# Row scores over the full array, a new order of first transfers, and layer 1 over whole tiles in a fused attention and feed-forward kernel

## Chip, cores, metric

One core of a Trainium2 chip. The metric is the device time of one execution in microseconds; the kernel before was timed three times.

## What is computed

For 8 batches of 512 tokens with 256 features: attention with 16 heads of 16, softmax over all keys and a triangular mask after it, a residual and a layer norm; a second residual and norm; then a gated feed-forward network with ternary weights, and a last norm. Cut to what matters:

```python
qk = einsum('bhqd,bhkd->bhqk', q, k) / sqrt(s)      # s = 512, 16 heads of 16
p = softmax(qk, axis=-1) * triu(ones((s, s)))       # masked after the softmax
x = embedded + einsum('bhqk,bhkd->bhqd', p, v)      # then a norm with gamma, beta
x = layernorm(x0 + attn(x0))
h = silu(tlin(x, w1)) * tlin(x, w2)                 # 256 -> 1024, twice
h = gelu(tlin(h, h1)); h = gelu(tlin(h, h2))        # 1024 -> 1024
x = layernorm(x + tlin(h, w3))                      # 1024 -> 256
```

## The kernel before

All engines run one hand-written program in program order, joined by semaphores. Each batch goes through attention, norms and feed-forward; the next batch's projections and row scores are placed into the feed-forward of the current one.

**Data split.** Values are kept as a rounded high half and a rest (`hi`, `lo`), so each feed-forward product is done twice. Q and K of a batch are stored to DRAM (`store_rows`) and loaded again as *stacks* `ST` of high and low halves, 64 rows for one head, four heads to a group (`QUAD`), four groups (`NQUAD`), two buffers (`group % 2`).

**Row scores** (`row_scores`, product L964) are there only for the maximum over keys of each query: TensorE makes scores with queries on partitions, VectorE takes the negated maximum (`row_max`, L714 for batches 1 to 7, L722 for batch 0). Here the stacks lie in a layout of their own (`load_rows`), two heads one above the other: rows 0 to 63 and rows 64 to 127 are two products in two halves of the array, into different banks. A *unit* is six or four such products (`SPANS`: three or two query tiles for each of the two sides), 12 units a batch, all on banks 0 to 5, each waiting for the maxima of the one before. Units stand at steps `UNIT_AT` (every 8 of the 128 steps of layers 2 and 3; a step is one k, that is a product with `hi` and one with `lo`), `beside` puts them in. For batch 0 there are 16 units of four, with two extra stacks `RST`.

**Turning the maxima** (`turn_max`, L980 and L981, at steps 54 and 108): 32 columns of maxima for 8 heads are transposed, split into high and low (`split_max`), stored (`store_max`) and loaded as rows 64 and 65 of the transposed stacks (`load_max`), whose partner rows are ones.

**Transposed scores** (`scores_T`, L995): products of 66 rows with keys on partitions, maximum already subtracted; ScalarE's exp reads them (L623). Groups 0 to 3 are loaded again in the transposed layout (`load_stacks(..., True)`). Then come the products with the values (L1014, L1021, L1027), normalizing (`take_z`), two norms (`first_norm`, `second_norm`) for each of four token tiles.

**Layer 1.** The normalized x is transposed in two parts, tokens 0 to 383 and 384 to 511 (`turn_x2`, L1043), and split (`take_x2_hi` on ScalarE, `split_x2` on VectorE). The first two of eight output tiles are computed in these two parts (`first_layer`, L1173), the others over 512 columns (L1078). Before them stand the projections of the next batch's K (L909) and V (L926). `keep_warm` (L972) issues products whose result is not used.

**Start.** SP's queue issues x, two weight matrices and all constants, ScalarE's queue the Q weights and three of the 1 MB pairs of feed-forward weights (`EARLY`), which ScalarE then tests for lost bits (`sum_lost`) and GpSimd rounds. Row scores of batch 0 need the stored Q and K rows; they are followed by the first transposed scores. The first transposed scores need the first half of the maxima.

**End.** The last norm waits for all four tiles and stores 512 KB at once.

Of the kernel before, what the change touches and what calls it, by code (L numbers as in the profile page):

```python
# [5 lines left out]
F32 = mybir.dt.float32  # L6
# [8 lines left out]
P = 128  # L15
# [14 lines left out]
EARLY = 3  # L30
# [16 lines left out]
FIRST_UNITS = H  # L47
SPANS = ((0, 3), (3, 6), (6, 8))
UNITS = NQUAD * len(SPANS)
# [4 lines left out]
def build_program(nc, x, xT, wqT, wkT, wvT, bqk, bv, gamma, beta, w1T, w2T, h1T, h2T, scales,  # L54
# [59 lines left out]
    RST, RST_f = both("first_stacks", [P, 2, QUAD, S], A + 8 * KB)  # L114
# [38 lines left out]
    qk_rows = nc.dram_tensor("qk_rows", [2, NQUAD, 2, HD, 2, 2 * S], F32, kind="Internal").ap()  # L153
    max_rows = nc.dram_tensor("max_rows_d", [2, H * QT * P], F32, kind="Internal").ap()

    with ExitStack() as ctx:
# [9 lines left out]
        first_rows_in = [sem("first_rows_in2"), sem("first_rows_in3")]  # L166
# [3 lines left out]
        rows_stored, max_stored, out_stored = sem("rows_stored"), sem("max_stored"), sem("out_stored")  # L170

        consts_set, masks_set = sem("consts_set"), sem("masks_set")
# [48 lines left out]
        LOADS_S, LOADS_T = 6 * 16, 7 * 16  # L221
        IN_PER_BATCH = 2 * LOADS_S + 2 * LOADS_T

        def after_stack(engine, b, group, transposed):

            loads_s = LOADS_S if b == 0 else 2 * LOADS_S
            had = (loads_s + (group // 2) * LOADS_T + LOADS_T) if transposed else (group // 2 + 1) * LOADS_S
            after(engine, stack_in[group % 2], b, IN_PER_BATCH, had if b == 0 else had - LOADS_S)

# [4 lines left out]

        UNIT_AT = {4 + 8 * u + 6 * (u // (UNITS // 2)): u for u in range(UNITS)}
        TURN_AT = {54: 0, 108: 1}
# [3 lines left out]
        def bank1(m, which):  # L240

            return 4 + (2 * m + 2 + which) % 4
# [9 lines left out]
        def units_of(b):  # L252

            return UNITS if b else FIRST_UNITS

        def after_units(engine, s, b, count, per_unit=1):

            done = FIRST_UNITS + (b - 1) * UNITS if b else 0
            if per_unit * done + count > 0:
                engine.wait_ge(s, per_unit * done + count)  # L260
# [4 lines left out]

        START_BANKS = (0, 4)
# [24 lines left out]

        @block.sync
        def _(sp):
# [3 lines left out]
            sp.dma_start(SC[:], scales.rearrange("p (n t) -> p n t", n=4)).then_inc(consts_in, 16)  # L297
            sp.dma_start(BV[:], bv.rearrange("(a d) -> a d", a=1).to_broadcast([P, D])).then_inc(consts_in, 16)
            sp.dma_start(ID[:], ident).then_inc(consts_in, 16)
            for t, src in ((GAM, gamma), (BET, beta), (S3, s3)):  # L300
                sp.dma_start(t[:], src.rearrange("(a d) -> a d", a=1).to_broadcast([P, D])).then_inc(consts_in, 16)

            def load_rows(stack, group, landed):

                for r1 in range(2):
                    sp.dma_start(stack(slice(r1, P, 2))[:, 0:2, :].rearrange("m pair s -> m (pair s)"),
                                 qk_rows[0, group].rearrange("side d part e -> (side d part) e")).then_inc(landed, 16)
                    for r2 in range(2):
                        sp.dma_start(stack(slice(2 * r1 + r2, P, 4))[:, 2:4, :].rearrange("m pair s -> m (pair s)"),
                                     qk_rows[1, group, :, :, r2, :].rearrange("side d e -> (side d) e")).then_inc(landed, 16)  # L310

            def load_stacks(b, group, transposed):


                n, back = 2 * H, 2 * QUAD * (group - 1)
                if group >= 2:
                    if transposed:
                        after(sp, scoredT, b, n, back)
                    else:
                        after_units(sp, scored, b, (group - 1) * units_of(b) // NQUAD)  # L320
                elif transposed:
                    after_units(sp, scored, b, (group + 3 if b else group + 1) * units_of(b) // NQUAD)
                else:
                    after(sp, scoredT, b, n, back)
                if group == 0 and not transposed:
                    after(sp, rows_stored, b, 4 * 16, 4 * 16)
                if not transposed:
                    load_rows(lambda rows: ST_f[rows, group % 2, 0, :, :], group, stack_in[group % 2])
                else:
                    for r2 in range(2):  # L330
                        sp.dma_start(ST_f[r2:SPLIT:2, group % 2, 0, :, :].rearrange("m (side pair) s -> m side (pair s)", pair=2),
                                     qk_rows[0, group].rearrange("side d part e -> (d part) side e")).then_inc(
                                         stack_in[group % 2], 16)
                    for r1 in range(2):
                        for r2 in range(2):
                            sp.dma_start(ST_f[2 * r1 + r2:SPLIT:4, group % 2, 1, :, :].rearrange(
                                "d (side pair) s -> d side (pair s)", pair=2),
# [926 lines left out]
```

## Time and profile before

| | |
|---|---|
| median of 3 runs | 1227.19 us (1227.16 to 1228.64) |
| the profiled execution | 1228.32 us, of it span 1226.6 us |
| TensorE busy | 1176.1 us, 96% |
| VectorE, GpSimd, ScalarE busy | 781.1, 561.6, 503.6 us |
| mean granted TensorE clock | 0.972 |

The span runs from the first to the last recorded instruction. Busy times of different engines overlap. The slices of the page cut the span into 40 equal parts, and a digit is the busy share in tenths. In a timeline a row can merge several equal instructions (x6), and the duration of a product reaches past the start of the next, since products are pipelined: what one costs is the distance between starts.

### The profile page before, as it was taken

What the parts mean: (1) busy time and instruction counts of PE and PEld (TensorE: products, weight loads), DVE (VectorE), ACT (ScalarE), POOL (GpSimd) and SP (SyncE); (2) the same over time, 40 slices, a digit from 0 to 9 for tenths busy, and PEclk for the clock granted to TensorE, in tenths of its full rate; (3) what the DMA queues carried; (4) which work ended last, traced back from release to release, by engine and by line L of the source; (5) the groups of instructions that cost most, each with busy time, mean ns of one, the idle gap of its engine ahead of it and who ended that gap; (6) DMA issues with size and microseconds to landing.
All of it is one profiled execution on the core that took longest, in us unless ns stands there. A gap on an engine that the chain in (4) does not pass through costs nothing.

```text
span 1226.6 us, 18621 instructions
## 1 busy us (share of the span) xinstructions
PE 1176.1 (96%) x7446; PEld 819.2 (67%) x7446; DVE 781.1 (64%) x1135; ACT 503.6 (41%) x676; POOL 561.6 (46%) x502
## 2 busy tenths in 40 slices
PE   5589999999999999999999999999999999999997
PEld 3244777657775677757777587756778577775886
DVE  3937666578646786477664786466864777748412
ACT  5366411664127621475116641276213751155310
POOL 4347522565236642376224652356423752246432
PEclk8569999999999999999999999999999999999999
DMA  8951322413234222233214132342222432141000
GB/s 297 339 150 52 123 71 72 113 48 114 68 77 105 106 67 71 62 97 138 71 49 117 53 121 64 86 106 93 80 71 53 106 138 70 37 104 37 1 1 18
DMA packets 44845, 111.74 MB, mean 91 GB/s; under 512 B 7952, under 2 KB 19600, under 8 KB 44688
## 3 DMA queue, kind: packets, MB, share of 16 engines
q1 hardware_dynamic: 40576, 98.68, 28.0%
q10 hardware_dynamic: 4176, 11.80, 2.8%
q8 instruction: 61, 1.00, 0.3%
q14 instruction: 32, 0.26, 0.1%
HBM read 88.95 MB, written 21.50 MB: 90 GB/s over the span
## 4 chain that ended last, share of the span: by engine, by line
PE 86%; DMA 4%; issue 3%; POOL 3%; DVE 3%; SPq 1%; ACT 0%; POOLq 0%; DVEq 0%; ACTq 0%
PE PS L1078 51%; PE PS L995 9%; PE PS L964 6%; PE PS L1014 5%; PE PS L909 4%; PE PS L1173 3%; PE PS L1021 2%; PE PS L926 2%; PE PS L1027 2%; DVE neg_max L722 2%; POOL diag_probs L500 1%; DMA max_rows_d<-max_rows 1%; DMA s_b<-s_dram 1%; DMA x_tok<-x_dram 1%; POOL rstd L513 1%
## 5 line engine op out<-in xcount | busy, mean ns | idle before, releaser
L714 DVE TENSOR_REDUCE neg_max<-PS 128x3 f32<-128x1536 f32 x168 | 257.6, 1575 | 61.2 <-PE PS L964 61.2
L487 POOL TENSOR_TENSOR hidA_lo<-hidA_full,hidA_hi 128x512 fp32r<-128x512 f32 x128 | 174.2, 1361 | 244.6 <-DVE hidA_hi L877 186.7
L623 ACT ACTIVATE probsT<-PS 128x1024 f32<-128x1024 f32 x256 | 248.1, 1021 | 83.3 <-PE PS L995 83.3
L1078 PE MATMUL PS<-hidA_hi,g 128*128 128x512 f32 x512 | 205.6, 402 | 0.0
L1078 PE MATMUL PS<-hidC_hi,g 128*128 128x512 f32 x512 | 203.9, 398 | 0.0
L1078 PE MATMUL PS<-hidA_lo,g 128*128 128x512 f32 x512 | 200.0, 391 | 0.0
L1078 PE MATMUL PS<-hidC_lo,g 128*128 128x512 f32 x512 | 199.8, 390 | 0.0
L500 POOL TENSOR_TENSOR diag_probs<-probsT,mask 128x512 f32<-128x512 f32 x120 | 156.8, 1311 | 59.8 <-PE PS L1078 31.1
L487 POOL TENSOR_TENSOR hidC_lo<-hidC_full,hidC_hi 128x512 fp32r<-128x512 f32 x64 | 82.4, 1288 | 194.4 <-DVE hidC_hi L877 194.4
L995 PE MATMUL PS<-stacks 66*128 66x512 f32 x512 | 154.6, 424 | 5.6 <-DMA stacks<-max_rows_d 5.4
L646 ACT ACTIVATE hidC_full<-PS,scales 128x512 f32<-128x512 f32 x64 | 44.2, 690 | 239.4 <-PE PS L1078 239.4
L646 ACT ACTIVATE hidA_full<-PS,scales 128x512 f32<-128x512 f32 x64 | 44.1, 689 | 224.9 <-PE PS L1078 224.9
L1078 PEld LDWEIGHTS PS<-hidA_hi,g 128*128 128x128 f32 x512 | 96.5, 188 | 37.1 <-issue 15.4
L1078 PEld LDWEIGHTS PS<-hidC_hi,g 128*128 128x128 f32 x512 | 96.1, 188 | 32.3 <-issue 12.8
L995 PEld LDWEIGHTS PS<-stacks 66*128 66x128 f32 x512 | 86.5, 192 | 44.5 <-issue 21.3
L1078 PEld LDWEIGHTS PS<-hidC_lo,g 128*128 128x128 f32 x512 | 96.2, 188 | 19.0
L1078 PEld LDWEIGHTS PS<-hidA_lo,g 128*128 128x128 f32 x512 | 96.3, 188 | 18.4
L964 PE MATMUL PS<-stacks 64*128 64x512 f32 x480 | 83.9, 448 | 18.6 <-issue 11.8
L1014 PE MATMUL PS<-probsT,ones_col 128*32 128x512 f32 (+3 forms) x1024 | 96.3, 448 | 4.9 <-issue 2.6
L877 DVE CAST hidA_hi<-hidA_full 128x512 fp32r<-128x512 f32 x64 | 27.3, 427 | 107.5 <-ACT hidA_full L646 107.5
L964 PEld LDWEIGHTS PS<-stacks 64*128 64x128 f32 x480 | 39.8, 193 | 55.4 <-issue 23.9
L1078 PE MATMUL PS<-x2T_hi,w 128*128 128x512 f32 x192 | 75.2, 392 | 0.0
(114 smaller groups left out, 1734.8 us busy)
## 6 DMA issues: line engine op xcount, KB each, us to landing
stacks<-qk_rows SPq DMA_DIRECT2D x124, 256.0 KB
stacks<-qk_rows SPq DMA_DIRECT2D x248, 128.0 KB
qk_rows<-qk_hi SPq DMA_DIRECT2D x16, 512.0 KB, 2.7
qk_rows<-qk_lo SPq DMA_DIRECT2D x16, 512.0 KB, 2.8
xT_sb<-xT_dram SPq DMA_DIRECT2D x8, 512.0 KB, 4.2
g_raw<-h1T_dram ACTq DMA_DIRECT2D x4, 1024.0 KB, 12.4
g_raw<-h2T_dram ACTq DMA_DIRECT2D x4, 1024.0 KB, 16.8
x_tok<-x_dram SPq DMA_DIRECT2D x8, 512.0 KB, 5.5
```

Source lines behind the costliest of these rows:

```text
L487: nc.gpsimd.tensor_tensor(lo[:, m, :], full[:, m, :], hi[:, m, :], ALU.subtract).then_inc(lo_done, 1)
L500: nc.gpsimd.tensor_tensor(masked(s), PT[:, s % RING, :, kt * P:(kt + 1) * P], MASK[:].rearrange("p (a m) -> p a m", a=1).to_broadcast([P, ...
L623: nc.scalar.activation(PT[:, s % RING, 2 * pair:2 * pair + 2, :], PS[:, 2 * pair:2 * pair + 2, :], ACT.Exp, scale=SCALE).then_inc(exp_done, 1)
L646: nc.scalar.activation(full[:, m, :], PS[:, bank23(m), :], ACT.Gelu, scale=SC[:, layer, m:m + 1]).then_inc(gelu_done, 1)
L714: nc.vector.tensor_reduce(NEGM[:, group // 2, at + lo:at + hi], PS[:, 3 * side:3 * side + hi - lo, :], AX.X, ALU.max, negate=True).then_in ...
L877: nc.vector.tensor_copy(hi[:, m, :], full[:, m, :]).then_inc(hi_done, 1)
L909: ins = nc.tensor.matmul(PS[:, bank_qk(n), :], w[:, k, c * P:(c + 1) * P], XT[:, k, :], start=(k == 0), stop=(k == DT - 1))
L964: ins = nc.tensor.matmul(PS[:, base + apart * side + n, :], stack(pair)[rows, qt * P:(qt + 1) * P], stack(2 + pair)[rows, :], start=True, ...
L995: ins = nc.tensor.matmul(PS[:, j, :], ST[0:ROWS, g % 2, 1, j, kt * P:(kt + 1) * P], ST[0:ROWS, g % 2, 0, j, :], start=True, stop=True)
L1014: nc.tensor.matmul(PS[32 * j:32 * j + 32, bank, lo:S], ONE[:, 0:32], PT[:, s % RING, j, lo:S], start=(kt == 0), stop=False, skip_group_che ...
L1078: ins = nc.tensor.matmul(out, d if swapped else w, w if swapped else d, start=(k == 0 and part == 0), stop=(k == kts - 1 and part == 1))
L1173: ins = nc.tensor.matmul(PS[:, bank1(m, which), tokens], w[:, k, m * P:(m + 1) * P], d[:, k, tokens], start=(k == 0 and d is X2hi), stop=( ...
```

## The change

- Row scores read the same stacks as the transposed scores: one product of 66 rows over the full array for each head and query tile. The two rows for the maxima hold zeros at that time: set once by GpSimd, stored as `zero_rows`, and loaded again for the first two groups of each later batch. A unit is two products of one head, 32 units a batch, on three pairs of banks in turn, at every third step (`SLOT_AT`); slots 16 and 33 are the turnings. VectorE takes the maxima of two products in one instruction. All batches use the same scheme.
- The order of groups is 2, 3, 0, 1. The stacks of groups 0 and 1 stay and are used by the transposed scores, which only need their maxima loaded (`load_max`), so two of eight group loads a batch fall away. The first transposed scores now need the last half of the maxima.
- First transfers: constants go behind the first group's stacks on ScalarE's queue; two weight pairs early instead of three; Q rows are stored and loaded ahead of K rows; the first group's loads are shared by two queues. Batch 0's V is taken after the maxima. The product that sums lost bits, and the reading of its flag, are placed elsewhere.
- Layer 1: no parts any more except in the last batch; the second transpose of x stands between the value projections. In the last batch three tiles are begun on the first 384 tokens, with 13 instead of 20 keep-warm products, and `split_x2` of the first part comes within the last tile's first norm.
- The last norm and store go tile by tile.

```diff
-EARLY = 3
+EARLY = 2
-FIRST_UNITS = H
-SPANS = ((0, 3), (3, 6), (6, 8))
-UNITS = NQUAD * len(SPANS)
+ROW_ORDER = (2, 3, 0, 1)
+UNITS = H * QT // 2
+GROUP_UNITS = UNITS // NQUAD
+HALF_UNITS = UNITS // 2
+SLOTS = UNITS + 2
...
-        UNIT_AT = {4 + 8 * u + 6 * (u // (UNITS // 2)): u for u in range(UNITS)}
-        TURN_AT = {54: 0, 108: 1}
+        SLOT_AT = {4 + 3 * slot: slot for slot in range(SLOTS)}
...
+        def half_of(part):
+            return 1 - part
+        def slot_bank(b, slot):
+            return ((0, 2, 4) if b else (4, 6, 0))[slot % 3]
...
             def start_attention(b):
                 store_max(b, 0)
-                load_stacks(b, 0, True)
                 store_max(b, 1)
+                load_max(b, 0)
+                load_max(b, 1)
...
-            store_rows(0)
-            for g in range(2):
-                load_stacks(0, g, False)
-            for g in range(2, NQUAD):
-                load_rows(lambda rows: RST_f[rows, g - 2, :, :], g, first_rows_in[g - 2])
-            load_stacks(0, 0, True)
-            load_stacks(0, 1, True)
-            store_max(0, 0)
-            load_max(0, 0)
-            load_max(0, 1)
+            sp.wait_ge(zeros_set, 1)
+            sp.dma_start(zero_rows.rearrange("r (h s) -> r h s", h=QUAD), ST_f[SPLIT:ROWS, 0, 0, :, :]).then_inc(zeros_stored, 16)
+            for a in range(2):
+                sp.wait_ge(qk_biased, (a + 1) * DT)
+                store_part(a, 0, QKhi_f)
+                sp.wait_ge(qk_split, (a + 1) * DT)
+                store_part(a, 1, QKlo_f)
+            sp.wait_ge(k_stored, 2 * 16)
+            for r2 in range(2):
+                load_k(sp, ROW_ORDER[0], 0, r2)
+            for group in ROW_ORDER[1:]:
+                load_stacks(0, group, False)
+            start_attention(0)
...
+                after_units(dve, scored, b, unit + 1)
+                nc.vector.tensor_reduce(NEGM[:, group // 2, at:at + 2], PS[:, bank:bank + 2, :], AX.X, ALU.max,
+                                        negate=True).then_inc(maxed, 1)
...
             def row_scores(b, slot):
+                elif slot >= 3:
+                    before = unit_of(slot - 3)
+                    if before is None:
+                        after(pe, max_split, b, 2, part_of(slot - 3) + 1)
+                    else:
+                        after_units(pe, maxed, b, before + 1)
+                for n in range(2):
+                    qt = 2 * pair + n
+                    ins = nc.tensor.matmul(PS[:, bank + n, :], ST[0:ROWS, group % 2, 0, j, qt * P:(qt + 1) * P],
+                                           ST[0:ROWS, group % 2, 1, j, :], start=True, stop=True)
...
-                after_units(pe, maxed, b, pairs, 2)
+                after_units(pe, maxed, b, (part + 1) * HALF_UNITS)
...
+                if slot >= SLOTS - 4 and unit_of(slot) is not None:
+                    after_units(pe, maxed, 0, unit_of(slot) - 1)
+                    keep_warm(slot_bank(0, slot), 1)
+                row_maxima(0, slot)
+            keep_warm(6, 10)
             scores_T(0, 0)
...
                 turn_x2(b, 0, last)
                 if not last:
                     project(b + 1, range(DT, 2 * DT))
-                    project_v(b + 1, range(QT))
+                    project_v(b + 1, range(QT // 2))
+                    turn_x2(b, 1, last)
+                    project_v(b + 1, range(QT // 2, QT))
                 else:
-                    keep_warm(7, 20)
-                if not general:
-                    first_layer(b, last, 0, 0)
-                turn_x2(b, 1, last)
-                if not general:
-                    first_layer(b, last, 1, 0)
-                    first_layer(b, last, 0, 1)
-                    first_layer(b, last, 1, 1)
+                    keep_warm(7, 13)
+                    if not general:
+                        first_layer(b, last, 0, 0)
+                        first_layer(b, last, 1, 0)
+                    turn_x2(b, 1, last)
+                    if not general:
+                        after(pe, exp_done, b, 2 * STEPS, 2 * STEPS)
+                        first_layer(b, last, 2, 0)
+                        for m in range(3):
+                            first_layer(b, last, m, 1)
...
+            for t in range(QT):
+                sp.wait_ge(out_ready, QT * (B - 1) + t + 1)
+                sp.dma_start(out[(B - 1) * S + t * P:(B - 1) * S + (t + 1) * P, :], OUT[:, t, :]).then_inc(out_stored, 16)
```

## Rows read from the trace of the kernel before

**Rows 1.** The page: busy time, and TensorE's tenths in 40 slices.

```profile
PE 1176.1 (96%) x7446; PEld 819.2 (67%) x7446; DVE 781.1 (64%) x1135; ACT 503.6 (41%) x676; POOL 561.6 (46%) x502
...
PE   5589999999999999999999999999999999999997
```

**Rows 2.** Windows: busy time of each engine, granted clock, DMA share, GB/s.

```profile
20.00:80.00 60.00, 32.39 (x106) 15.84 (x106) 39.51 (x39) 23.22 (x40) 20.82 (x21) 0.50 0.82 272
80.00:112.00 32.00, 31.32 (x331) 16.03 (x330) 19.76 (x35) 26.81 (x31) 26.59 (x25) 0.98 0.30 69
```

**Rows 3.** Timeline, TensorE, layers 2 and 3 of batch 2: start, duration, line.

```profile
434.70 0.39 PE L1078 MATMUL PS<-hidA_hi,g 128*128 128x512 f32 x1
...
441.38 0.96 PE L964 MATMUL PS<-stacks 64*128 64x512 f32 x6
...
446.12 0.73 PE L964 MATMUL PS<-stacks 64*128 64x512 f32 x4
...
450.64 0.97 PE L964 MATMUL PS<-stacks 64*128 64x512 f32 x6
...
471.52 0.39 PE L1078 MATMUL PS<-hidC_hi,g 128*128 128x512 f32 x1
...
505.81 1.09 PE L995 MATMUL PS<-stacks 66*128 66x512 f32 x4
506.73 0.28 PE L1078 MATMUL PS<-w,hidA_hi 128*128 128x256 f32 x1
```

**Rows 4.** Chain that ended last, feed-forward of the last batch.

```profile
1140.83 69.00 PE PS L1078 x304
```

**Rows 5.** Timeline, VectorE, first high half in layer 3.

```profile
472.44 0.43 DVE L877 CAST hidC_hi<-hidC_full 128x512 fp32r<-128x512 f32 x1 [0.24 <-ACT hidC_full L646]
```

**Rows 6.** Groups of instructions by shape: VectorE's maxima, busy us, mean ns.

```profile
L714 DVE TENSOR_REDUCE neg_max<-PS 128x3 f32<-128x1536 f32 x112 | 191.7, 1753 | 44.7 <-PE PS L964 44.7
...
L714 DVE TENSOR_REDUCE neg_max<-PS 128x2 f32<-128x1024 f32 x56 | 66.0, 1220 | 16.4 <-PE PS L964 16.4
```

**Rows 7.** Timeline, TensorE and VectorE, before and in layer 1 of batch 2.

```profile
415.56 3.62 PE L926 MATMUL PS<-wv,xT_sb 128*128 128x256 f32 x16
418.82 0.52 PE L1173 MATMUL PS<-x2T_hi,w 128*128 128x384 f32 x1
...
423.74 0.45 PE L1078 MATMUL PS<-x2T_hi,w 128*128 128x512 f32 x1
...
416.37 0.41 DVE L760 TENSOR_SCALAR x_tok<-x_tok,mean_var,rstd 128x256 f32<-128x256 f32 x1 [0.67 <-POOL rstd L513]
```

**Rows 8.** Start: SP's and TensorE's timeline, then the chain that ended last.

```profile
14.77 1.31 SPq L356 DMA_DIRECT2D qk_rows<-qk_lo  x2
...
28.34 2.07 PE L964 MATMUL PS<-stacks 64*128 64x512 f32 x8 [11.81 <-issue]
...
29.60 19.32 DVE neg_max L722 x17
49.45 16.40 DMA max_rows_d<-max_rows
65.87 4.60 DMA stacks<-max_rows_d
...
70.52 2.08 PE PS L995 x4
```

**Rows 9.** Timeline, TensorE: last scores of batch 0; two of batch 3.

```profile
110.45 1.20 PE L995 MATMUL PS<-stacks 66*128 66x512 f32 x4
...
517.84 1.20 PE L995 MATMUL PS<-stacks 66*128 66x512 f32 x4
...
541.31 1.19 PE L995 MATMUL PS<-stacks 66*128 66x512 f32 x4
```

**Rows 10.** Timeline, the last batch: layer 1 on TensorE, and SP's last store.

```profile
1135.82 0.44 PE L1173 MATMUL PS<-x2T_hi,w 128*128 128x384 f32 x1 [0.87 <-DVE x2T_lo L801]
...
1223.20 0.38 SPq L468 DMA_DIRECT2D out_dram<-out_tok  x1
```

More of the change, by code:

```diff
@@ L250, in bank_y, with after_units @@
             return 4 + (t + 2) % 4
[L252 to L260, printed above, removed]
+        def after_units(engine, s, b, count):
+            after(engine, s, b, UNITS, count)
         def bank_qk(n):
             return (6, 7, 0, 1)[n]
-        START_BANKS = (0, 4)
         def masked(s):
@@ L312, in load_stacks @@
[L312 to L337, printed above, removed]
-                                         qk_rows[1, group, :, :, r2, :].rearrange("side d e -> d side e")).then_inc(
-                                             stack_in[group % 2], 16)
-                    if b:
-                        load_max(b, group)
@@ L343, in load_max @@
+                        load_k(sp, group, r1, r2)
+                if transposed:
+                    load_max(b, group)
             def load_max(b, group):
[L345 to L346 removed]
+                    after(sp, max_stored, b, 32, 16 if half_of(0) == group // 2 else 32)
                     sp.dma_start(ST_f[SPLIT:ROWS, group % 2, 0, :, :],
@@ L829, in last_norm, with attention @@
                         normalize(X, OUT, t).then_inc(out_ready, 1)
-            def attention(b, first):
+            def attention(b, first, last):
                 if not first:
@@ L842, in attention @@
                     take_z(b, g)
-                    first_norm(b, g)
+                    first_norm(b, g, last and g == NQUAD - 1)
                     second_norm(b, g)
             def body(b, first, last):
-                attention(b, first)
-                split_x2(b)
+                attention(b, first, last)
+                if not last:
+                    split_x2(b, 0)
+                split_x2(b, 1)
                 if not last:
@@ L950, in stack @@
-                def stack(place):
-                    return RST[:, group - 2, place, :] if b == 0 and group >= 2 else ST[:, group % 2, 0, place, :]
-                if b:
-                    lo, hi = SPANS[unit % len(SPANS)]
-                    products = [divmod(n, QT) for n in range(lo, hi)]
-                    base, apart = 0, 3
-                else:
-                    i, half = divmod(unit, 2)
-                    products = [(i % 2, 2 * half), (i % 2, 2 * half + 1)]
-                    base, apart = banks[unit % len(banks)], 2
@@ L961, in row_scores @@
-                for n, (pair, qt) in enumerate(products):
-                    for side in range(2):
-                        rows = slice(side * SPLIT, (side + 1) * SPLIT)
-                        ins = nc.tensor.matmul(PS[:, base + apart * side + n, :],
-                                               stack(pair)[rows, qt * P:(qt + 1) * P], stack(2 + pair)[rows, :],
-                                               start=True, stop=True)
+                elif slot >= 3:
+                    before = unit_of(slot - 3)
+                    if before is None:
+                        after(pe, max_split, b, 2, part_of(slot - 3) + 1)
+                    else:
+                        after_units(pe, maxed, b, before + 1)
@@ L1085, in product @@
                         nc.tensor.drain().then_inc(chunk_used, 1)
-                for m in range(0 if general else 2, HT):
+                for m in range(3 if last and not general else 0, HT):
                     for which, w in ((0, W1), (1, W2)):
```

303 lines of the change are left out of this document (176 added, 127 removed).

## Prediction

> **What bounds the kernel now.** I read the page first: TensorE is busy 1176.1 of a 1226.6 us span, and the only slices in which it is not full are the first three and the last [rows 1]. So two things count: what TensorE issues in a full stretch, and the chain of waits at the two ends. The granted clock is at half level (0.50, 1.2 GHz) from 20 to 80 us, in which TensorE worked only 32.39 of 60 us, and near full (0.98) from 80 to 112 us [rows 2]. Then I read the timeline of one middle batch: the step from one product to the next is constant there, with no idle time, so an added or removed instruction in layers 2 and 3 costs or gives back its own issue time, times 7, since row scores for the next batch run beside the feed-forward of batches 0 to 6.
>
> **Row scores, before.** Layers 2 and 3 last from 434.70 to 505.81, 71.11 us [rows 3]. The last batch has no row scores beside it; there 304 feed-forward products are one link of the chain that lasts 69.00 us, 0.227 us each [rows 4]. 256 of them are 58.1 us, so row scores and the two turnings of the maxima cost 13.0 us a batch. By parts: from one unit to the next lie 16 products (3.63 us) and the unit. With a unit of six products the distance is 4.74 us (441.38 to 446.12), with a unit of four 4.52 us (446.12 to 450.64) [rows 3]. So a unit of six costs 1.11 us, one of four 0.89. Two more products cost 0.22 us, the time of one full product: the two 64-row halves do run together. But each of the 12 units also carries 0.45 us that is not work. 8 x 1.11 + 4 x 0.89 = 12.4 us, and 0.6 is left for the turnings.
>
> **Row scores, after.** 32 units of two products of 66 rows, one after the other. The nearest row is the transposed scores of the same stacks: four such products between feed-forward products take 505.81 to 506.73, 0.92 us, 0.23 each, and nothing is lost before or after them [rows 3]. 64 x 0.23 = 14.7 us, with turnings 15.3, so +2.2 us a batch. Bounds: 0.227 each gives +2.0; a lost 0.03 us at each unit gives +3.2.
>
> Here the Trainium skill speaks against the change. What the row shows comes first: a pair of half-row products in 0.22 us, and 0.45 us lost per unit [rows 3]. "TensorEngine Tiling (Array Packing)", sections "The Solution" and "Key Properties", says that a contraction of at most 64 rows may run up to twice as fast on row tiles, and that a change of tiling mode drains the engine. By the first half alone the old units would be 32 x 0.22 = 7.0 us and the change would cost 7.7 us a batch, 54 us in all; the trace agrees with both halves together, and the drains give most of it back.
>
> **New waits at the turnings.** A turning now stands three steps behind the last unit of its half (n = 49 then 52; 100 then 103); before it stood ten or more. VectorE works in order: the copy of the high half of a layer's tile starts 0.92 us after the tile's last product (471.52, next tile begins; 472.44, copy) and lasts 0.43 [rows 3, 5]. The tile of step 49 begins at 0: copy done at 1.35; the maximum of two products lasts 1.22 [rows 6], so it is done at 2.6. TensorE reaches the turning at 0.45 + 0.46 + 1.36 = 2.27. It waits about 0.4 us, and I add 0.1 for the restart. For the second turning the unit of step 100 is taken from 2.9 to 4.1, and TensorE comes at 4.09: 0.1. Behind the waiting transpose stand the layer's own products. Sum 0.5 to 0.6 (none to 1.5). Nothing else waits: between a unit and the use of its banks again lie 18 products and three units, 5.5 us, against at most 2.7 of VectorE; its maxima cost 32 x 1.22 = 39 us a batch against 8 x 2 x 1.75 + 4 x 2 x 1.22 = 38 [rows 6], so it stays below 80% of these 73 us. The last maxima now go through memory after step 103: 25 steps, 11.3 us, are left before the next scores, against about 5 for split, store and load. Row scores in the steady part: +2.7 us a batch, **+18.9 us** in 7 (bounds +14 and +30).
>
> **Layer 1 over whole tiles.** Before, 16 products of 384 columns, two transposes and 16 products of 128 columns take 418.82 to 423.74, 4.92 us [rows 7]. After, the transposes (0.14, and 0.1 for the change of kind) stand among the value projections, and 16 products of 0.227 follow, with the same first gap of 0.19: 4.06. With 0.06 of a gap behind, 0.9 saved a batch, **-6.4 us** in 7 (bounds -8 and -3). The cover: the transposes need the fourth tile normalized, done at 416.8, while the first half of the value projections (from 415.56) ends near 417.2 [rows 7]; one short operation each of ScalarE and VectorE follows, and the other half of the projections, 1.6 us, hides them. If that cover were gone it would cost at most 1 us a batch. The low halves for layer 2 come about 1 us earlier too, so that wait stays hidden.
>
> **The start.** Before: the last row store is issued at about 15.4 us (the second of the merged pair); the stack loads start when it has landed, and row scores begin at 28.34; VectorE takes maxima without pause (17 in 19.32 us, 1.14 each), and TensorE's first transposed scores come at 70.52 behind a store that took 16.40 and a load of 4.60 us, queued behind the big loads of the transposed stacks [rows 8]. After: constants and one megabyte of weights leave the first queue, the Q rows are stored and loaded on their own, and the last four loads are split over two queues. I put the last rows in memory at 18.4, the last load of the first group issued at 20.4 and the first row score at 23.3, 5 us earlier. Maxima: 24.5 + 32 x 1.14 + 1.9 (the first turning, during which VectorE finds nothing ready) = 62.9. But the maxima needed first are now the last ones made: turning and split 1.1, store 2, load 3 (no big loads ahead, weights beside) end at 69, only 1.5 us earlier (bounds: 63.5, if every hand-over is short; 72, if the third group's stack is late). SP's added 16 KB transfer of zeros is 0.45 us of issue in an idle queue, and the constants that ScalarE's queue now issues come long before the first turning needs them.
>
> From the first scores to the last of batch 0 is 70.52 to 110.45, 39.9 us for 15 steps; ten middle steps take 517.84 to 541.31, 2.35 each, so 35.2 would do [rows 8, 9]. The excess is the half clock of the first steps, ScalarE's four weight tests, and a wait of about half a microsecond for the sum of lost bits. The keep-warm products, ten of them before the first scores, should bring the full clock sooner; ScalarE's share stays. I take -2.8 (bounds 0 and -4.3), and -0.5 for the sum's product, moved past that wait. Start together **-4.8 us** (bounds +2 and -12).
>
> **The end.** In the last attention the low halves of the first three tiles are taken before the fourth's second norm, so first-layer products need not wait 0.87 us until 1135.82 [rows 10], and seven of twenty keep-warm products (1.7 us) give way to work. TensorE gains about 2, but the high and low halves from VectorE and GpSimd, in series for eight tiles, are then late for layer 2: **-1.3** (bounds 0 and -2.5). The last norm goes tile by tile: the last VectorE work ends near 1221.5 instead of 1223.2, and a 128 KB store follows 512 KB (issue at 1223.20, end 1226.6) [rows 10]: **-2.2** (bounds -1 and -3).
>
> **Sum.** +18.9 - 6.4 - 4.8 - 1.3 - 2.2 = +4.2 us. The profiled execution took 1228.32, 1.13 above the median of 1227.19; on its own it gives 1232.5, on the median 1231.4.
>
> **Rivals.**
> - *The start gives all it can.* The chain reaches the first scores at 63.5 and the clock is full: -7.0 - 4.3 - 0.5 = -11.8 instead of -4.8, so 1224.4: faster. For it: TensorE is idle 11.8 us before the first row score, and the new order has nothing large ahead of the maxima. Against: the DMA is saturated there (share 0.82 over 20 to 80 us [rows 2]) and 36.5 us of maxima stay in series. It decides once the start saves more than 11.5 us.
> - *The turnings wait for nothing.* If the copy ahead of the last maximum is earlier than I reckon, 0.55 x 7 = 3.9 us fall away: 1227.5, no difference. For it: the wait is the difference of five durations, and half of it is a tenth of a microsecond in each. Against: the copy cannot precede its own tile's end.
> - *VectorE sets the pace between units.* If maxima arrive late at every tile, not only at turnings, 0.1 us for each of 16 tiles and 1 us at each turning, 3.6 a batch in place of 0.6: +21, 1252. Against: the 5.5 us of slack above.
> - *The fixed 0.45 us belongs to any unit, not to the mode.* 32 x 0.45 x 7 = +101: 1332. The four-product row at 505.81 speaks against it; a quarter of it would be 1257.
>
> **How the numbers follow.** Forecast 0.54, with its own range 1228 to 1236; start gives all 0.20; turnings hidden 0.14; VectorE's pace 0.08; a fixed cost 0.04. Within 0.2% (2.5 us, about what a measurement can tell from no change) lie the case of hidden turnings, a fifth of the forecast's and a bit of the first rival: 0.25 same, 0.22 faster, 0.53 slower. The range 1222.5 to 1238 leaves out the last two and the tail of the first. Predicted 1231.4.
>
> **What would show it.** Products of the row scores 0.23 us apart with no gap around them; layers 2 and 3 at 73.8 us in place of 71.1; a wait of TensorE for the maxima at the first turning, 0.4 us; layer 1's first two tiles in 3.8; first row score at 23 us, first transposed scores at 69; each middle batch 1.8 us longer. I am wrong if it does not grow, or if the first transposed scores come before 65.

## The result: 1.1% slower, and the profile after

The changed kernel takes 1241.64 us (median of 4 runs, 1240.77 to 1242.15), the kernel before 1227.91 in the runs beside it: ratio 1.0111, 95% interval 1.0095 to 1.0127, 13.7 us slower. I had forecast slower, but 1231.4 with an upper end of 1238. The profiled execution took 1242.15, its span 1240.4 us against 1226.6.

The page, with busy time and TensorE's slices, against [rows 1]:

```profile
PE 1207.0 (97%) x7342; PEld 872.0 (70%) x7342; DVE 786.2 (63%) x1194; ACT 505.4 (41%) x676; POOL 565.7 (46%) x506
...
PE   6889999999999999999999999999999999999998
```

TensorE is busy 31 us longer with fewer matmuls, and still full in nearly every slice.

**Layers 2 and 3.** The timeline of TensorE in batch 2, against [rows 3]:

```profile
438.49 0.39 PE L1124 MATMUL PS<-hidA_hi,g 128*128 128x512 f32 x1
...
442.17 0.63 PE L1006 MATMUL PS<-stacks 66*128 66x512 f32 x2
442.63 0.40 PE L1124 MATMUL PS<-hidA_hi,g 128*128 128x512 f32 x1
442.87 0.40 PE L1124 MATMUL PS<-hidA_lo,g 128*128 128x512 f32 x1
...
444.01 0.63 PE L1006 MATMUL PS<-stacks 66*128 66x512 f32 x2
...
469.73 0.39 PE L1124 MATMUL PS<-hidA_lo,g 128*128 128x512 f32 x1
470.18 0.19 PE L1021 MATMUL PS<-ones_f,qk_square_sum 128*1 128x1 f32 x2
...
501.28 0.40 PE L1124 MATMUL PS<-hidC_lo,g 128*128 128x512 f32 x1
501.60 0.33 PE L1022 MATMUL PS<-ident_sb,neg_max 128*128 128x128 f32 x1
...
513.14 1.09 PE L1043 MATMUL PS<-stacks 66*128 66x512 f32 x4
```

From 438.49 to 513.14 are 74.65 us, against 71.11 before: +3.54 a batch. The products of a unit are 0.23 apart and no idle time stands beside them, but the next unit comes after 1.84 to 1.87 us (mean 1.854), where eight full products of 0.2267 would take 1.81. Ahead of the first turning 0.45 us pass instead of 0.227, ahead of the second 0.32.

**Layer 1.** Same engine, same batch, against [rows 7]:

```profile
420.26 1.89 PE L980 MATMUL PS<-wv,xT_sb 128*128 128x256 f32 x8
421.99 0.38 PE L1091 MATMUL PS<-ident_sb,x_tok 128*128 128x128 f32 x2
422.21 1.89 PE L980 MATMUL PS<-wv,xT_sb 128*128 128x256 f32 x8
423.75 0.58 PE L1124 MATMUL PS<-x2T_hi,w 128*128 128x512 f32 x1
424.17 0.40 PE L1124 MATMUL PS<-x2T_lo,w 128*128 128x512 f32 x1
```

From 420.26 to layer 2 at 438.49 are 18.23 us, 19.14 before: -0.91 a batch.

**The start.** The chain that ended last, from 16 to 71 us (start, duration, what), against [rows 8]:

```profile
16.43 4.72 DMA qk_rows<-qk_lo
...
21.84 4.05 DMA stacks<-qk_rows
25.90 0.25 issue
26.15 8.33 PE PS L1006 x16
...
46.82 11.62 DMA stacks<-qk_rows
58.44 0.04 issue
58.49 1.23 PE PS L1006 x2
...
69.13 1.24 DVE neg_max L743
```

VectorE's timeline there:

```profile
27.45 9.14 DVE L743 TENSOR_REDUCE neg_max<-PS 128x2 f32<-128x1024 f32 x8 [20.58 <-PE PS L1006]
...
49.04 9.14 DVE L743 TENSOR_REDUCE neg_max<-PS 128x2 f32<-128x1024 f32 x8 [2.01 <-PE PS L1006]
59.75 5.75 DVE L743 TENSOR_REDUCE neg_max<-PS 128x2 f32<-128x1024 f32 x5 [1.56 <-PE PS L1006]
66.17 2.50 DVE L743 TENSOR_REDUCE neg_max<-PS 128x2 f32<-128x1024 f32 x2 [0.67 <-PE PS L1006]
```

TensorE's timeline, third group, the end of the start, last scores of batch 0 and the flag:

```profile
47.78 8.28 PE L1006 MATMUL PS<-stacks 66*128 66x512 f32 x16 [1.38 <-DMA stacks<-qk_rows]
58.49 4.88 PE L1006 MATMUL PS<-stacks 66*128 66x512 f32 x10 [2.43 <-DMA stacks<-qk_rows]
...
70.54 4.61 PE L1013 MATMUL PS<-w 128*128 128x512 f32 x10
75.11 1.60 PE L1043 MATMUL PS<-stacks 66*128 66x512 f32 x4
...
111.19 1.19 PE L1043 MATMUL PS<-stacks 66*128 66x512 f32 x4
...
118.98 1.12 PE L963 MATMUL PS<-xT_sb,wq 128*128 128x512 f32 x2 [2.04 <-DVE inexact L897]
```

The row scores begin at 26.15, 2.2 us earlier than before, but the maxima end at 70.4 and the transposed scores begin at 75.11, 4.6 us later than before. VectorE idles 3.3 us around the first turning (45.71 to 49.04, of it 0.6 of split), 1.56 before the fourth group and 1.1 beside the keep-warm products. The last scores come 36.1 us after the first (39.9 before). The granted clock beside them: 1.00 from 76 us on, 1 us behind the first transposed scores; before it was 0.50 until 80 and 0.63 from 80 to 82 us, so full some 11 us behind them.

**The end.** VectorE's last work and SP's stores, against [rows 10]:

```profile
1236.84 1.26 DVE L789 TENSOR_SCALAR out_tok<-x_tok,mean_var,rstd 128x256 f32<-128x256 f32 x3
```

```profile
1233.44 5.16 SPq L481 DMA_DIRECT2D out_dram<-out_tok  x4
```

From the first product of W3 (1226.12, before 1209.65) to the end are 14.3 us, 16.95 before.

**The account, in spans.** Layers 2 and 3: 7 x 3.54 = +24.8. Layer 1: 7 x -0.91 = -6.4. Start: +4.6 to the first transposed scores, -3.8 in the first attention, +0.1 from the last scores to the value projections, where the span of layer 1 begins (16.9 after, 16.8 before): +0.8. Last batch, from the first keep-warm product (1145.86, before 1127.88) to W3: -1.5. End: -2.7. Sum +15.0 against +13.8 seen. The 1.2 between lie in the attentions of batches 1 to 7. From first to last transposed scores most take 40.4 us in both traces, but batches 1, 5 and 7 took 0.9 to 1.4 longer before, and batches 4 and 5 took 1.0 and 0.7 longer after. I have no cause for these.

### The profile page after: what moved, and what is told of

It is laid out like the page before. It is cut to its first block, busy times and chain, and to the rows that moved or that the text cites. A ratio compares the mean times of both kernels' runs of the same rounds, so it can differ in the third digit from the quotient of the medians.

```text
span 1240.4 us, 18457 instructions
## 1 busy us (share of the span) xinstructions
PE 1207.0 (97%) x7342; PEld 872.0 (70%) x7342; DVE 786.2 (63%) x1194; ACT 505.4 (41%) x676; POOL 565.7 (46%) x506
## 4 chain that ended last, share of the span: by engine, by line
PE 88%; POOL 3%; DVE 3%; DMA 2%; issue 2%; ACT 1%; SPq 1%; POOLq 0%; DVEq 0%; ACTq 0%
PE PS L1124 50%; PE PS L1006 10%; PE PS L1043 9%; PE PS L1062 5%; PE PS L963 5%; PE PS L1069 3%; PE PS L980 2%; PE PS L1075 2%; POOL diag_probs L516 2%; DMA stacks<-qk_rows 1%; DVE neg_max L743 1%; ACT probsT L643 1%; PE PS L1013 1%; POOL rstd L529 1%; PE PS L1091 1%
## 5 line engine op out<-in xcount | busy, mean ns | idle before, releaser
L743 DVE TENSOR_REDUCE neg_max<-PS 128x2 f32<-128x1024 f32 x256 | 310.6, 1222 | 103.8 <-PE PS L1006 102.5
L1124 PE MATMUL PS<-hidA_hi,g 128*128 128x512 f32 x512 | 201.9, 394 | 0.4 <-POOL hidA_lo L503 0.4
L1124 PE MATMUL PS<-hidC_hi,g 128*128 128x512 f32 x512 | 201.3, 393 | 0.0
L1006 PE MATMUL PS<-stacks 66*128 66x512 f32 x512 | 174.9, 431 | 12.8 <-DMA stacks<-qk_rows 12.8
L1043 PE MATMUL PS<-stacks 66*128 66x512 f32 x512 | 152.5, 418 | 1.0 <-ACT probsT L643 1.0
L1006 PEld LDWEIGHTS PS<-stacks 66*128 66x128 f32 x512 | 102.2, 205 | 46.3 <-DVE neg_max L743 11.1
L1043 PEld LDWEIGHTS PS<-stacks 66*128 66x128 f32 x512 | 84.3, 189 | 40.5 <-issue 21.5
L1124 PE MATMUL PS<-x2T_hi,w 128*128 128x512 f32 x244 | 96.4, 395 | 0.0
## 6 DMA issues: line engine op xcount, KB each, us to landing
g_raw<-h2T_dram ACTq DMA_DIRECT2D x4, 1024.0 KB, 14.3
```

Source lines behind the costliest of these rows:

```text
L743: nc.vector.tensor_reduce(NEGM[:, group // 2, at:at + 2], PS[:, bank:bank + 2, :], AX.X, ALU.max, negate=True).then_inc(maxed, 1)
L1006: ins = nc.tensor.matmul(PS[:, bank + n, :], ST[0:ROWS, group % 2, 0, j, qt * P:(qt + 1) * P], ST[0:ROWS, group % 2, 1, j, :], start=True, ...
L1043: ins = nc.tensor.matmul(PS[:, j, :], ST[0:ROWS, g % 2, 1, j, kt * P:(kt + 1) * P], ST[0:ROWS, g % 2, 0, j, :], start=True, stop=True)
L1124: ins = nc.tensor.matmul(out, d if swapped else w, w if swapped else d, start=(k == 0 and part == 0), stop=(k == kts - 1 and part == 1))
```

## Experiments

Each was timed against the kernel before; I give the ratio with its interval. The changed kernel is at 1.0111 [1.0095, 1.0127].

### The parts that gain, alone

```diff
-                for m in range(0 if general else 2, HT):
+                for m in range(2 if last and not general else 0, HT):
...
-                    project_v(b + 1, range(QT))
+                    project_v(b + 1, range(QT // 2))
+                    turn_x2(b, 1, last)
+                    project_v(b + 1, range(QT // 2, QT))
...
```

> The kernel before, with layer 1 of batches 0 to 6 over whole tiles and nothing else: the transposes of the fourth tile stand among the value projections, and the first two tiles of layer 1 are no longer cut into 384 and 128 columns. My sum: 0.9 us saved in each of 7 batches, -6.4 us against the kernel before, about 1221.5. Rival, that the 0.91 us a batch seen between the value projections and layer 2 of the changed kernel comes from its other row scores: no change here.

Measured 1222.75 us (1220.18 to 1224.91), 0.9959 [0.9946, 0.9973], -5.0 with an interval of -6.6 to -3.3, which holds the -6.4 expected. In its trace one batch takes 142.53 us in place of 143.45, -0.92: the gain of layer 1 does not need the new row scores.

The next one keeps the row scores and the start of before, and takes over everything else.

> The changed kernel's layer 1, last attention, last norm and place of the lost-bits sum, with the row scores and the start of the kernel before. If the loss of 13.7 us lies in row scores and start alone, this version is faster than the kernel before by the gains of its parts: 6.4 for layer 1, about 5 for the last attention and the end (the trace of the changed kernel shows 5.0 from the last batch's mark to the end, layers 2 and 3 of batch 6 taken out), 0 to 0.5 for the flag: 1215.5 to 1218. Rival, that the gains at the end hang on the new row scores or the other order of loads: 1220 or more.

Measured 1219.45 us, 0.9930 [0.9916, 0.9944]: -8.6, 1.5 to 4 us short of what I expected. Its last batch and end are those of the changed kernel. But its granted clock is still 0.54 from 84 to 92 us, 1.00 in the version above, though TensorE was busy in both from 72 us on. So its first attention took 42.6 us from first to last transposed scores, 39.5 in the version above. What made the clock rise later I don't know. And moving the lost-bits sum gains nothing: VectorE's flag is then late, and TensorE waits 2.0 us for it in place of 2.1 elsewhere. So row scores and start together cost about 22 us of the change by the timed runs; by the spans above it is 25.6, and most of the difference is this version's slower first attention.

### What a unit costs between feed-forward products

Two units at one step:

```diff
-        SLOT_AT = {4 + 3 * slot: slot for slot in range(SLOTS)}
+        SLOT_AT = {}
+        for slot in range(SLOTS):
+            SLOT_AT.setdefault(4 + 3 * slot if slot == SLOTS - 1 else 4 + 6 * (slot // 2), []).append(slot)
```

> The changed kernel with two units at the same step of layers 2 and 3: 17 places of interruption instead of 34, every sixth step, the products and maxima the same. Theory: each interruption of the feed-forward costs a fixed 0.03 us beyond its products (0.49 a unit instead of 0.46), so 16 fewer in each of 7 batches give 3 to 3.5 us, and the wait at the first turning, which now stands six steps behind its last unit, 0.1 to 0.2 a batch more: -3.5 to -5 against the changed kernel, about 1237. Rival: the feed-forward products themselves run slower (0.233 us apart instead of 0.227) because VectorE's reads and the stacks' loads lie beside them, however the units are placed: at most -1.

And the two products of a unit at neighbouring steps:

```diff
...
+                    if n in SECOND_AT:
+                        row_scores(b + 1, SECOND_AT[n], (1,))
+                    if n + 1 in SECOND_AT:
+                        row_scores(b + 1, SLOT_AT[n], (0,))
...
```

> The changed kernel with the two products of 30 of 32 units a batch put at neighbouring steps, two feed-forward products between them: 30 more interruptions in each of 7 batches, the products and maxima the same. Theory (a fixed 0.03 us for each interruption): +6 us against the changed kernel, 1248. Rival (the feed-forward is slower by what lies beside it): within 1 us of the changed kernel.

Paired: 1234.88 us, 1.0058 [1.0045, 1.0072], 6.5 below the changed kernel, more than either theory gave. Spread: 1241.99 us, 1.0113 [1.0098, 1.0129], no change, as the rival had it. The two answers contradict a fixed 0.03 us, so I took mean steps from one start to the next, by position, from the timelines of batches 0 to 6 (the last column is the next experiment's kernel):

```
mean step, us            changed   paired (4 products)   spread (1 product)   128 rows
the unit's products       0.467         0.930                  0.234            0.453
1st product behind        0.234         0.235                  0.235            0.227
2nd                       0.233         0.231                  0.231            0.227
3rd                       0.234         0.233                                   0.227
4th to 6th, mean          0.228         0.226                                   0.227
```

A feed-forward product elsewhere takes 0.2267. So each of the next two or three products behind an insertion is some 0.005 to 0.009 slower, and each inserted one 0.006 to 0.007: 0.040 us for a unit of two, 0.039 for a pair of units, 0.023 for a single product. The price is paid once for a stretch of inserted products, and two or four of them cost the same. That makes 1.2 us a batch in the changed kernel, 0.6 less when paired, 0.2 more when spread. The spans agree: spread's layers 2 and 3 were 0.2 longer. Paired also gained 0.13 at the first turning, where 0.32 us are left of 0.45; in all its layers 2 and 3 are 0.76 shorter.

Then the rows themselves: the same products, over 128 rows.

```diff
-            nc.gpsimd.memset(ST_f[SPLIT:ROWS, :, 0, :, :], 0.0).then_inc(zeros_set, 1)
+            nc.gpsimd.memset(ST_f[SPLIT:P, :, 0, :, :], 0.0).then_inc(zeros_set, 1)
...
-            nc.vector.memset(ST_f[SPLIT:ROWS, :, 1, :, :], 1.0).then_inc(consts_set, 1)
+            nc.vector.memset(ST_f[SPLIT:P, :, 1, :, :], 1.0).then_inc(consts_set, 1)
...
-                    ins = nc.tensor.matmul(PS[:, bank + n, :], ST[0:ROWS, group % 2, 0, j, qt * P:(qt + 1) * P],
+                    ins = nc.tensor.matmul(PS[:, bank + n, :], ST[0:rows, group % 2, 0, j, qt * P:(qt + 1) * P],
...
```

> The changed kernel with the steady row scores over all 128 rows of the stacks instead of 66; rows 66 to 127 hold zeros on one side and ones on the other, so the sums are the same. In the changed kernel's middle batches a unit's two products take 0.230 us each and the first three feed-forward products behind it 0.234, against 0.2267 for a feed-forward product elsewhere: 0.033 us a unit, 1.05 a batch. Theory: this is the price of passing between 66 and 128 rows; with all products alike it goes, layers 2 and 3 take 1.05 us less, -7 us in 7 batches, 1234. Rival: it comes from the other weights and buffers of an inserted unit, or from its semaphores, whatever the rows: no change.

Measured 1233.37 us beside 1230.19 for the kernel before in these runs: 1.0027 [1.0016, 1.0038], some 10 us below the changed kernel. Its timeline of TensorE, batch 2:

```profile
437.70 0.62 PE L1007 MATMUL PS<-stacks 128*128 128x512 f32 x2
438.15 0.39 PE L1125 MATMUL PS<-hidA_hi,g 128*128 128x512 f32 x1
438.38 0.39 PE L1125 MATMUL PS<-hidA_lo,g 128*128 128x512 f32 x1
...
439.51 0.62 PE L1007 MATMUL PS<-stacks 128*128 128x512 f32 x2
439.97 0.39 PE L1125 MATMUL PS<-hidA_hi,g 128*128 128x512 f32 x1
```

Six products now take 1.36 us and the unit 0.45. Layers 2 and 3 are 1.22 us shorter than in the changed kernel in every batch, 8.5 in all, and the excess of a unit and the products behind it, 1.2 of them, is gone at every position. (I had expected 1.05, having taken the unit's own products at 0.230 each; they take 0.234.) So it came from the step between products of 66 and of 128 rows, not from the insertion, semaphores or VectorE's reads, which are all as they were.

Last, all scores over 128 rows, and the same paired:

```diff
-                        ins = nc.tensor.matmul(PS[:, j, :], ST[0:ROWS, g % 2, 1, j, kt * P:(kt + 1) * P],
-                                               ST[0:ROWS, g % 2, 0, j, :], start=True, stop=True)
+                        ins = nc.tensor.matmul(PS[:, j, :], ST[:, g % 2, 1, j, kt * P:(kt + 1) * P],
+                                               ST[:, g % 2, 0, j, :], start=True, stop=True)
```

> As the version with steady row scores over all 128 rows, and the row scores of the start and all transposed scores over 128 rows too (zeros against ones in rows 66 to 127). In attention four transposed scores take 1.13 us from the first to the next group of products, 0.28 each, where four at 0.227 would take 0.91: 0.22 us are lost in each of 16 steps of 8 batches. Theory A, the loss is the passage between 66 and 128 rows: up to -28 us against the version before it, and at least what that passage cost in the feed-forward, 0.03 a step, -4. Theory B, the loss belongs to the products of 32 and 16 columns that surround the scores, and the rows add nothing to it: 0 to -4.

> The same with two units at the same step of layers 2 and 3. If the price of an interruption is only that of the passage between 66 and 128 rows, nothing of it is left and pairing gives back no more than the wait at the first turning, 0.13 to 0.3 us a batch: -1 to -2 against the unpaired version. If interruptions cost something of themselves, 16 fewer at 0.014 to 0.025 give 1.6 to 2.8 more.

Measured 1230.80 us, 1.0015 [1.0004, 1.0027], and 1229.11 us, 1.0005 [0.9992, 1.0019]. Neither step can be told from none by its interval. The timeline of the first, in attention:

```profile
535.88 1.20 PE L1044 MATMUL PS<-stacks 128*128 128x512 f32 x4
537.01 1.06 PE L1063 MATMUL PS<-probsT,ones_col 128*32 128x512 f32 x8
```

Four transposed scores take 1.13 us as before, whatever their rows: that the rows add nothing, as theory B had it, is shown; that the products of 32 and 16 columns around the scores are the cause is not, since no version changed them. With 128 rows pairing shortens layers 2 and 3 by 0.18 us a batch, no more than the wait at the turning; an interruption costs nothing of itself.

One thing changed at the start. With the same row scores over 128 rows the granted clock is 0.75 from 20 to 40 and 0.76 from 40 to 60 us (0.76 and 0.76 in the paired version), against 0.54 and 0.50 where they have 66 rows. TensorE was then busy for 11.4 and 11.5 of 20 us, with 66 rows for 14.0 and 14.1. It brought little, since VectorE sets the pace of these maxima: the first transposed scores come at 73.03 instead of 75.03.

### The start

A second buffer for the second group, so that the fourth group's loads needn't wait:

```diff
+    RST, RST_f = both("first_stacks", [P, 2, QUAD, S], C)
...
-            for group in ROW_ORDER[1:]:
+            for group in (ROW_ORDER[1], ROW_ORDER[3], ROW_ORDER[2]):
```

> The changed kernel with a buffer of its own for the second group's stack at the start, so that the fourth group's loads go out at once and not when the second group's products are done; the third group's still wait for the first's. Theory: late stacks cost 1.4 us behind the first turning and 1.6 us at the fourth group. With both gone the first transposed scores begin at 72 instead of 75.1 and the time falls by 3 us; if only the fourth group's wait goes, by 1.5. Rival: the loads only move the wait, since the queue and the DMA are full with weights: the third group comes later by what the fourth comes earlier, and the time stays within 1 us.

Measured 1239.61 us, 1.0097 [1.0082, 1.0113]: no measurable gain. Its timeline of TensorE:

```profile
47.66 13.93 PE L1020 MATMUL PS<-stacks 66*128 66x512 f32 x26 [2.31 <-DMA stacks<-qk_rows]
```

The wait at the fourth group is gone and the one at the third has grown from 1.38 to 2.31: the rival is mostly right. From first row score to first transposed score pass 48.05 us in place of 48.96.

Weights held back (`stack_in[...]` awaited at 2 * LOADS before the next three pairs are issued):

> The changed kernel with the three megabytes of weights that follow the first stack held back until the third group's stack has landed. Theory: that stack's loads, issued from 34.5 us and used at 47.8, are slow because weights fill the DMA (share 0.8 and more); without them they land within 5 us, the wait of 1.4 us behind the turning goes, and the maxima end 1.4 earlier. The fourth group's loads then meet the weights, so its 1.6 us stay or grow. The weights themselves come some 10 us later, and with them ScalarE's tests of them, so the first attention starts later: the whole is slower, +3 to +8. Rival: the loads wait for their issue (for the first group's products), not for the DMA: the third group comes no earlier.

Measured 1243.69 us, 1.0115 [1.0098, 1.0132], no slower than the changed kernel by what the runs can tell, where I had expected 3 to 8 us; the timeline of TensorE:

```profile
45.81 8.26 PE L1006 MATMUL PS<-stacks 66*128 66x512 f32 x16
57.36 2.93 PE L1006 MATMUL PS<-stacks 66*128 66x512 f32 x6 [3.29 <-DMA stacks<-qk_rows]
```

No wait for the third group, 3.29 for the fourth, and the last scores of batch 0 at 114.44 in place of 111.19. So the third group's loads, issued at the same time as before, were late because of the weights beside them.

One pair of weights less ahead of the rows (`EARLY = 1`), and no keep-warm products in the last units:

> The changed kernel with one megabyte of feed-forward weights ahead of the rows instead of two. Theory: the store of the low halves of K took 4.7 us because these weights share the DMA with it; it lands in about 3, the first row score comes at 24.5 instead of 26.15, and the third and fourth groups' stacks come earlier as well: first transposed scores at 73, -2 us. Rival: a store takes 4.7 us by itself, or the weights shifted behind the stacks delay the third group instead: no change.

> The changed kernel without the three keep-warm products in the last units of the start; the ten ahead of the first transposed scores stay. Theory: VectorE, which sets the pace of the maxima, idles 1.1 us for them, so the first transposed scores come 1.1 us earlier and the time falls by about 1. Rival: what they cost comes back as a later full clock in the first attention: no change.

1240.57 us, 1.0106 [1.0090, 1.0122], and 1240.11 us, 1.0099 [1.0084, 1.0114]. In the first one the row store still takes 4.6 us (issued 15.79, loads from 20.38) and the row scores begin at 25.69, 9.9 us after that issue (9.7 in the changed kernel): the megabyte taken away is not its cause. What else lies there is the loads of the Q rows, issued at 15.70 on the other queue; I did not try that alone. In the second the maxima go 1.4 us faster and the first transposed scores come 1.6 us sooner after the first row score (47.4 us in place of 48.96); in the timed runs that stays under what they can tell.

### A faster version

The version without the new row scores, with one line moved at the start:

```diff
             load_stacks(0, 0, True)
-            load_stacks(0, 1, True)
             store_max(0, 0)
+            load_stacks(0, 1, True)
```

> The version with the row scores and start of the kernel before and the other parts of the changed one, with the store of the first half's maxima issued ahead of the loads of the second transposed stack. Before, that store was issued at 49.45 us and took 16.40 us behind those loads. Theory: it lands some 8 us earlier, and the first transposed scores, which waited 6.2 us for it and its load, come up to 4 us earlier: -2 to -4, about 1216. Rival: then they wait for the second transposed stack, or for the maxima themselves, which end near 64 us: less than 1 us gained.

Measured 1213.40 us, 0.9885 [0.9866, 0.9905]: 14 us faster than the kernel before. SP's queue, then TensorE's timeline:

```profile
49.81 0.33 SPq L371 DMA_DIRECT2D max_rows_d<-max_rows  x1
...
58.64 0.57 SPq L349 DMA_DIRECT2D stacks<-max_rows_d  x2
```

```profile
68.31 2.08 PE L1031 MATMUL PS<-stacks 66*128 66x512 f32 x4 [2.87 <-DMA stacks<-max_rows_d]
```

The load of the maxima is issued at 58.64 instead of behind a store that ended at 65.85, and the first transposed scores come 39.6 us after the first row score (42.2 before, 42.9 in the version without the move). The load itself now takes 9.6 us (4.6 before), so less is gained than the store's 7.6. Against the version without the move the runs differ by 5.5 us, 3.3 of them this; in its trace the rest comes with the clock, which is 1.00 from 80 us on and not only from 92, so that the last scores of batch 0 come at 107.07 for 114.70.

> The version with the store of maxima moved ahead (1213.4), with two of the changed kernel's start edits besides: two megabytes of weights ahead of the rows instead of three, and the first group's loads split over two queues. Theory: the last row store lands at 21 instead of 22.3 us and the loads are issued in 2 us instead of 3.1; first row score at 26.5 instead of 28.7, and since VectorE's maxima follow without pause, the first transposed scores come as much earlier: -2, 1211.4. Rival: the weights lost ahead come back as late tests on ScalarE before the first attention: no change.

Measured 1212.88 us, 0.9855 [0.9835, 0.9876]; the interval overlaps that of the last version, so no gain is shown. The timeline of TensorE:

```profile
64.02 2.08 PE L1040 MATMUL PS<-stacks 66*128 66x512 f32 x4 [1.63 <-DMA stacks<-max_rows_d]
...
69.90 1.71 PE L1040 MATMUL PS<-stacks 66*128 66x512 f32 x3 [2.74 <-ACT probsT L632]
```

The first scores come 4.3 us earlier than in the last version, the second ones wait for ScalarE, which still tests weights, and the last scores of batch 0 come at 107.95, against 107.07: the rival.

## Why the prediction was wrong

- **What bounds the kernel** held: what TensorE issues in layers 2 and 3 counted seven times, and both ends counted as chains.
- **Units of row scores: the step that failed.** I put them at 14.7 us a batch since "nothing is lost before or after them". The row for that showed four such products and where the next one began, not the two or three behind it, and it was followed by products of another width. Measured: 15.0 for the units' own products, and 0.8 more in the products behind them. "A lost 0.03 us at each unit" stood in my bounds and was nearly the right value (0.034). The 128-row version shows the cause, the change between 66 and 128 rows.
- **Turnings.** I added 0.5 to 0.6 us of waits for 0.6 of turning. My own durations give 0.3 for the first, not 0.4 (2.57 less 2.27), and none for the second. Measured is 0.13 of wait at the first, none at the second, and 0.8 to 0.9 for turnings and waits together in place of 1.15. With the units: +3.54 instead of +2.7 a batch, 5.9 us in all. The rival of hidden turnings was nearly right by itself.
- **Layer 1.** -0.9 a batch predicted, -0.91 measured, -0.92 alone.
- **The start: the other term that failed**, -4.8 predicted, +0.8 measured. First row score at 26.15 instead of 23.3: I let the last rows land at 18.4, they landed at 21.15, and why the store took 4.7 us stays open. Maxima end at 70.4 instead of 62.9: 2.95 us from the later begin and 4.5 on the way, of which 4.1 are three things that I had not priced, or only as a bound ("if the third group's stack is late"): the third group 1.4 late, the fourth 1.6, keep-warm 1.1. I had read the DMA share of 0.82 as an argument against the best case only, not as the price of stacks that can be loaded only when a buffer is free. The trip of the maxima through memory was 1.3 shorter than I said and hidden behind ten keep-warm products. The first attention, with the full clock 1 us and not 11 us behind its first scores, gave -3.8 for -2.8. The moved sum of lost bits gave nothing: the wait for it became a wait for its flag.
- **The last batch and the end.** -1.5 for -1.3, and -2.7 for -2.2.
- **The rule on row tiles.** The Trainium skill ("TensorEngine Tiling (Array Packing)", "Theoretical Speedup" and "Key Properties") had said that the change gives up a speedup and that a change of tiling mode drains. Both are borne out by the units before (0.45 us lost, yet 3.5 us a batch cheaper). In attention the products around the scores are of 32 and 16 columns, and there four scores take 1.13 us for 0.91 with either number of rows; that agrees with the rule, but no version tests it. The rule does not cover the loss between 66 and 128 rows: by the list in the Trainium skill ("TensorEngine Tiling (Array Packing)", "Available Configurations") row tiles have 64 or 32 rows, so 66 rows and 128 both fall under no row tiling.

Terms: 5.9 of row scores and 5.6 of the start, less 0.7 at the end and 1.2 unexplained in the attentions, and 0.7 by which the kernel before was slower beside it: 10.3, for a miss of 10.2.

## What to carry to other kernels

An inserted instruction's price is the distance between the same neighbours with and without it, over several instructions behind it; a row that stops at the next start hides part of the price. Where a contraction is a little over half the array, fill the rest with zeros before giving it a shape of its own among full products. When a stage reuses double buffers while something large fills the DMA, price each reload by what its queue and its neighbours carry, and send small stores ahead of large loads on the same queue.

## What the runs showed of the hardware

- Two products of 66 rows between products of 128 rows were each 0.007 us slower, and so was each of the next three; with zeros to 128 rows all take 0.2267. It was worth 1.22 us a batch in the traces, 8.5 in seven; the timed ratios differ by 10 us.
- With row scores of 128 rows instead of 66 at the start, the granted clock was 0.75 and not 0.54 from 20 to 40 us, and 0.76 and not 0.50 from 40 to 60.
- Four scores among products of 32 columns took 1.13 us over 66 rows and over 128.
- A 32 KB store of maxima took 16.40 us behind a megabyte of loads on its queue; issued ahead of these it took 8.8 us (49.81 to 58.62), and the load behind it 9.6 instead of 4.6.
